# Layer 0's expert rows sorted on the chip: one expert on each tile of sorted rows in place of eight experts on each tile of tokens

## The reference

```python
x = L0_attn_x
xn = _layernorm(x, axis=-1)
x = x + _L0_attn_ref(xn, ...) + _L0_ffn_ref(xn, ...)   # linear attention, 4 heads of 32; 8 experts, top 2
xn = _layernorm(x, axis=-1)
x = x + _L1_attn_ref(xn, ...) + _L1_ffn_ref(xn, ...)   # 16 causal heads of 64; 8 experts, grouped top 2
```

```python
xn = rms_norm(x, norm_scale)
scores = (xn @ w_router.T).astype(jnp.float32)
scores_topk, idx = jax.lax.top_k(scores, TOP_K)
weights = jax.nn.softmax(scores_topk, axis=-1)
...
up = moe_linear(xf, ids, w_up)          # row i gets w_up[ids[i]]: 128 -> 512
u, gate = jnp.split(up, 2, axis=-1)
h = u * jax.nn.silu(gate)
down = moe_linear(h, ids, w_down)       # 256 -> 128
out = jnp.sum(down.reshape(B, S, TOP_K, D) * weights[..., None], axis=-2)
```

## Time and profile before

| | us |
|---|---|
| median of 3 runs (lowest, highest) | 782.28 (782.05, 784.48) |
| the profiled execution | 782.97 |
| its span, first to last instruction | 781.2 |
| busy: PE, DVE, ACT, POOL | 730.0, 594.1, 477.9, 345.8 |
| mean granted TensorE clock | 0.989 of full speed |

### The profile page before, as it was taken

The page is one execution under the profiler, slowest core; times in us unless marked ns, Lnnn a source line. Parts: engine busy times, 40 slices in busy tenths (PEclk is TensorE's granted clock), DMA queues, the critical chain, the costliest instruction groups (busy, mean ns, idle before and its releaser), DMA issues.

```text
span 781.2 us, 17355 instructions
## 1 busy us (share of the span) xinstructions
PE 730.0 (93%) x5473; PEld 595.4 (76%) x5473; DVE 594.1 (76%) x2233; ACT 477.9 (61%) x1276; POOL 345.8 (44%) x699
## 2 busy tenths in 40 slices
PE   2876799999999999999999999999999999999997
PEld 1765588887887878877888878777888778878875
DVE  3694987788777887778877887778877787877774
ACT  3536665676657665576656766576655756576554
POOL 3264552392425742274523924257522843257111
PEclk9997899999999999999999999999999999999999
DMA  9400000000000000000000000000000000000000
GB/s 319 170 7 1 0 3 1 1 2 14 2 2 1 2 15 2 2 1 15 2 2 1 2 15 1 3 1 1 16 2 2 1 8 2 2 1 1 8 2 8
DMA packets 6027, 12.49 MB, mean 16 GB/s; under 512 B 480, under 2 KB 4864, under 8 KB 5296
## 3 DMA queue, kind: packets, MB, share of 16 engines
q1 hardware_dynamic: 5936, 11.37, 4.2%
HBM read 10.32 MB, written 1.05 MB: 15 GB/s over the span
## 4 chain that ended last, share of the span: by engine, by line
PE 74%; DVE 13%; issue 4%; ACT 4%; POOL 3%; DMA 1%; DVEq 0%; SPq 0%; POOLq 0%; ACTq 0%
PE b_y L1256 12%; PE b_simA L1304 7%; PE b_pv L1333 7%; PE b_gate L1119 5%; PE b_prT L1316 4%; PE b_y L1289 4%; PE b_gate L1121 3%; PE b_gate L1120 3%; DVE th L967 3%; PE b_up L1119 3%; PE b_up L1121 3%; PE b_up L1120 2%; DVE th L975 2%; PE b_pv L1340 2%; PE b_simB L1177 2%
## 5 line engine op out<-in xcount | busy, mean ns | idle before, releaser
L527 POOL CAST pn<-prb 128x4 fp32r<-128x4 f32 x256 | 45.7, 208 | 228.1 <-DVE prb L1051 107.1
L692 ACT ACTIVATE prb<-prb,mneg 128x130 f32<-128x130 f32 (+1 forms) x256 | 113.8, 449 | 51.7 <-DVE mneg L1066 51.7
L669 ACT ACTIVATE th<-b_gate 128x512 f32<-128x512 f32 x128 | 76.5, 598 | 111.1 <-PE b_gate L1121 109.7
L1256 PE MATMUL b_y<-down,th 128*128 128x128 f32 x1024 | 140.1, 280 | 0.9 <-DVE th L975 0.5
L1256 PEld LDWEIGHTS b_y<-down,th 128*128 128x128 f32 x1024 | 126.3, 192 | 15.1 <-issue 11.5
L967 DVE SCALAR_TENSOR_TENSOR th<-th,b_gate 128x512 f32<-128x512 f32 x128 | 87.5, 684 | 34.8 <-ACT th L669 34.1
L474 POOL TENSOR_TENSOR rn<-ss,halves 128x8 f32<-128x8 f32 x64 | 105.0, 1644 | 7.0 <-DVE ss L896 7.0
L975 DVE TENSOR_TENSOR th<-b_up,th 128x512 f32<-128x512 f32 x128 | 88.1, 689 | 10.9 <-PE b_up L1121 8.1
L1119 PE MATMUL b_gate<-xf_h,up_h 128*128 128x256 f32 x256 | 85.4, 334 | 5.8 <-DVE th L967 5.4
L1119 PE MATMUL b_up<-xf_h,up_h 128*128 128x256 f32 x256 | 79.2, 309 | 0.0
L1304 PE MATMUL b_simA<-qkT 64*128 64x130 f32 (+1 forms) x256 | 75.9, 377 | 1.5 <-DVE mneg L1066 0.8
(11 more groups left out here) (200 smaller groups left out, 1748.6 us busy)
## 6 DMA issues: line engine op xcount, KB each, us to landing
qkT<-w_up SPq DMA_DIRECT2D x1, 2048.0 KB, 9.2
down<-w_dn SPq DMA_DIRECT2D x2, 1024.0 KB, 15.3
qk<-w_up SPq DMA_DIRECT2D x1, 2048.0 KB, 14.9
x_in<-x SPq DMA_DIRECT2D x8, 128.0 KB, 2.6
qkT<-w_qk SPq DMA_DIRECT2D x1, 1024.0 KB, 5.0
result<-acc SPq DMA_DIRECT2D x8, 128.0 KB, 1.9
...
```

The source lines that it names most:

```text
L669: nc.scalar.activation(th[e % 2][:], b_gate[:], ACT.Tanh, scale=0.5).then_inc(*act_moe[layer](f"th{e}"))
L692: nc.scalar.activation(prb[p % 2][:, i, 0:n], prb[p % 2][:, i, 0:n], ACT.Exp, scale=-1.0, bias=mneg[:, qt, h:h + 1], accum_out=lsum[:, qt, ...
L1256: ins = nc.tensor.matmul(b_y[:, t * D:(t + 1) * D], th[e % 2][:, a * S + t * P:a * S + (t + 1) * P], down[layer][:, e, a], start=(a == 0), ...
```

## The change

Layer 0 no longer goes by batch up to its experts. At the start all sixteen tiles of tokens are normalised and routed at once, on DVE, with the count of rows before each row by a scan and a matmul. The two rows of every token get positions in a table `sorted_rows` in device memory, where each expert's rows begin at a multiple of 128: 40 tiles (5120 rows, zeroed first), each of one expert. POOL writes the rows there by indirect DMA; layer 0's attention (`mixing`) is computed meanwhile for all batches. Then PE, ACT and DVE work through PAIRS = 20 pairs of tiles; the expert of a tile is read from `slot_expert` into a register that addresses the weights. The results go to `expert_rows`, from which four indirect DMAs per batch fetch each token's two rows again. The rounds keep heads, layer 1's experts (now at EXPERT_AT, every second step from 2 to 16) and front1 with other places; front0 is gone from them. The high and low parts of the up weights now have one buffer for both layers, so that layer 1's are split after the pairs, in front1 of batch 0.

The rounds, the constants of the order:

```diff
+EXPERT_AT = [2, 4, 6, 8, 10, 12, 14, 16]
...
-            for b in range(0, B - 2):
-                in_round(b, steps)
-            in_round(B - 2, steps, f0=False)
-            in_round(B - 1, steps, m0=False, f0=False, f1=False)
+            return lambda b, p: step(b, p) if b >= 0 else None
+
+        def front(front1, i):
+
+            return lambda b, p: front1(b + 1, 2 * p + i) if b + 1 < B else None
+
+        def all_rounds(*steps):
+            for b in range(-1, B):
+                for p in range(ROUND):
+                    for step in steps:
+                        step(b, p)
+        PROJ_AT = [10 + 3 * n for n in range(8)]
+        SQUARE_AT = [k + 1 for k in PROJ_AT]
+        ROOT_AT = [k + 2 for k in PROJ_AT]
```

SP: zeroing, and the loads and stores of pairs:

```diff
+            sp.wait_ge(zero_set, 1)
+            flat_rows = sorted_rows.rearrange("(p r) d -> p (r d)", p=P)
+            for at in range(0, ROWS * D // P, 2 * HD1):
+                n = min(2 * HD1, ROWS * D // P - at)
+                sp.dma_start(flat_rows[:, at:at + n], zeros[:, 0:n]).then_inc(zero_in, 16)
...
+            def load_rows(s):
+
+                if s >= 4:
+                    sp.wait_ge(pair_pe["turn"], s - 3)
+                sp.dma_start(rows_in[s % 4], sorted_rows[2 * s * P:2 * (s + 1) * P].rearrange("(t p) d -> p t d", p=P))\
+                    .then_inc(rows_loaded[s % 4], 16)
+
+            sp.wait_ge(scattered, 16 * 2 * TILES)
+            for s in range(4):
+                load_rows(s)
+            sp.dma_start(flat(xf_all), w_up1[:, 0:2 * QUARTER]).then_inc(up1_in[0], 16)
+            for s in range(PAIRS):
+                if s + 4 < PAIRS:
+                    load_rows(s + 4)
+                sp.wait_ge(pair_act["out"], s + 1)
+                sp.dma_start(expert_rows[2 * s * P:2 * (s + 1) * P].rearrange("(t p) d -> p t d", p=P), rows_out[s % 2])\
+                    .then_inc(rows_stored[s % 2], 16)
```

POOL: scatter, and the gathers inside the rounds:

```diff
+            pool.wait_ge(zero_in, 16 * ZEROINGS)
+            pool.wait_ge(xf_set, 2)
+            pool.wait_ge(*ROUTED("pos"))
+            for k in range(2):
+                for i in range(TILES):
+                    nc.gpsimd.indirect_dma_start(out=sorted_rows, out_offset=bass.IndirectOffsetOnAxis(ap=pos[:, k, i:i + 1], axis=0),
+                                                 in_=xf_all[:, i], in_offset=None).then_inc(scattered, 16)
+
+            pool.wait_ge(scattered, 16 * 2 * TILES)
...
+            def take_rows(b):
+
+                if b == 0:
+                    pool.wait_ge(nv_set, 1)
+                    for i in range(2):
+                        pool.wait_ge(rows_stored[i], 16 * PAIRS // 2)
+                pool.wait_ge(*dve_f1.at(b - 2, "x1"))
+                for t in range(T):
+                    for k in range(2):
+                        nc.gpsimd.indirect_dma_start(out=taken_rows[b % 2][:, t, k], out_offset=None, in_=expert_rows,
+                                                     in_offset=bass.IndirectOffsetOnAxis(ap=pos[:, k, T * b + t:T * b + t + 1], axis=0))\
+                            .then_inc(rows_taken[b % 2], 16)
+                pool.wait_ge(rows_taken[b % 2], 16 * 2 * T * (b // 2 + 1))
...
-                if 28 <= k < 36:
-
-                    n = k - 28
+                if k in (1, 4):
+                    inverse_std(b, k // 4)
+                if k == 12 and b + 1 < B:
+                    take_rows(b + 1)
+                for n in [n for n in range(8) if k == ROOT_AT[n]]:
+
                     w, t, g = piece_of(n)
                     hs = slice(g * HALF, (g + 1) * HALF)
                     pool.wait_ge(*dve_f1.at(b, f"floor{n}"))
                     nc.gpsimd.tensor_tensor(rn[:, w, t, hs], ss[:, w, t, hs], halves[:, 0:HALF], ALU.pow).then_inc(*pool_f1(f"rn{n}"))
-                    if not (isinstance(b, int) and b == 0):
+                    if b:
                         pool.wait_ge(*pool_f1.at(b, f"rn{n}"))
                         unit_vectors(nc.gpsimd, n)
```

ACT in the pair stage (its four pieces and their order):

```diff
+            def pair_input(s):
+
+                act.wait_ge(pair_pe["turn"], s + 1)
+                if s >= 2:
+                    act.wait_ge(pair_pe["up"], s - 1)
+                nc.scalar.activation(pair_h[s % 2][:], pair_T[s % 2][:, 0:2 * P], ACT.Copy).then_inc(pair_act["xh"], 1)
...
+            def pair_gate(s):
+
+                act.wait_ge(pair_pe["up"], s + 1)
+                if s >= 2:
+                    act.wait_ge(pair_pe["hidT"], s - 1)
+                nc.scalar.activation(pair_th(s), pair_half(s, 1), ACT.Tanh, scale=0.5).then_inc(pair_act["th"], 1)
...
+            for s in range(2):
+                pair_input(s)
+            for s in range(PAIRS + 2):
+                if s < PAIRS:
+                    pair_gate(s)
+                if s + 2 < PAIRS:
+                    pair_input(s + 2)
+                if s >= 2:
+                    pair_out(s - 2)
+                if 1 <= s <= PAIRS:
+                    pair_hidden(s - 1)
```

PE: routing's count, and the pair stage:

```diff
+            pe.wait_ge(*ROUTED("rank"))
+            ends = rank[:, :, TILES - 1]
+            nc.tensor.matmul(b_count[:, 0:E], below, ends, start=True, stop=True)
+            nc.tensor.matmul(b_count[:, E:2 * E], ones, ends, start=True, stop=True).then_inc(counted, 1)
...
+            def pair_ups(s):
+
+                pe.wait_ge(pair_dve["xl"], s + 1)
+                if s >= 2:
+                    pe.wait_ge(pair_dve["hid"], s - 1)
+                for t in range(2):
+                    e = pe.value_load(slot_expert[0:1, 2 * s + t:2 * s + t + 1], min_val=0, max_val=E - 1)
+                    tok = slice(t * P, (t + 1) * P)
+                    high = up_h[:, bass.ds(e, 1), :].rearrange("p e n -> p (e n)")
+                    ins = matmul3(pair_up[s % 2][:, t * 512:(t + 1) * 512], pair_h[s % 2][:, tok], pair_l[s % 2][:, tok],
+                                  high, up_l[:, bass.ds(e, 1), :].rearrange("p e n -> p (e n)"))
+                ins.then_inc(pair_pe["up"], 1)
...
+            def pair_down(s):
+
+                pe.wait_ge(pair_act["hidT"], s + 1)
+                if s >= 1:
+                    pe.wait_ge(pair_act["out"], s)
+                for t in range(2):
+                    e = pe.value_load(slot_expert[0:1, 2 * s + t:2 * s + t + 1], min_val=0, max_val=E - 1)
+                    for a in range(HB):
+                        ins = nc.tensor.matmul(b_rows[:, t * D:(t + 1) * D], hidT[s % 2][:, t * HB + a],
+                                               down[:, bass.ds(e, 1), a * D:(a + 1) * D].rearrange("p e n -> p (e n)"),
+                                               start=(a == 0), stop=(a == HB - 1), skip_group_check=True)
+                ins.then_inc(pair_pe["down"], 1)
...
+            pe.wait_ge(*ROUTED("slots"))
+            pe.wait_ge(up_lo[0], 4)
+            pe.wait_ge(dn0_in, 16)
+            for s in range(2):
+                pair_turn(s)
+            for s in range(PAIRS + 2):
+                if s < PAIRS:
+                    pair_ups(s)
+                if s + 2 < PAIRS:
+                    pair_turn(s + 2)
+                if s >= 2:
+                    pair_down(s - 2)
+                if 1 <= s <= PAIRS:
+                    pair_hidden(s - 1)
```

1322 lines of the change are left out of this document (713 added, 609 removed).

## The result

The changed kernel takes 886.91 us, median of four runs (882.98 to 894.74), against 782.38 (782.05 to 784.48): ratio 1.134, 95% interval 1.125 to 1.143. Slower was forecast, at 794 with a range up to 852; the time lies 93 us above the forecast and 35 above the range.

The account below looks back on a forecast made before the run. PE's work was taken to bound the full rounds, with chains setting start and end. First score at 230, plus rounds of 435, 70 and 57.6, gave 793, adjusted to 794 us; range 742 to 852.

Parts of the forecast that it names:

- A: Start, routing all tokens at once: loads, normalisations, logits and a DVE chain; positions stand at 33 us (bounds 30 to 38).
- B: Scatter: 32 indirect DMAs on POOL at 1.2 us each, 38.4, then landing of the last and first row load, 2.6 each.
- C: Pair stage: PE's work 3.5 us a pair plus 1.5 of register loads in the open, 5.0; 20 pairs make 100.
- D: First gathers after the pair stage: four indirect DMAs at 1.2 us and a landing of 2.6, 7.4 us.
- E: front1 of batch 0, alone: today's 32.5 us plus x1's additions 1.3 and the weight split 4, 37.8.
- F: Rounds: 63.2 us of PE work and present waits, plus 6.7 and 2.5; six with gathers 435, the one without 70.
- 7.4 against a lead of two steps: Next batch's gathers and landing in POOL's queue ahead of pn, delaying DVE's scores: 2.5 us a round (bounds 0 to 6).
- R2: Rival, slower still: indirect DMAs at 1.64 us and PE at 1.2 GHz for half the pair stage; 840 us, chance 0.20.
- 6.7 + 2.5: Added time a round: 6.7 us exposed while DVE holds the first three steps, 2.5 us of waiting for pn behind gathers.
- The last round: Final round, which had no layer-0 experts before either: taken as 57.6 us, as today.
- R1: Rival, not slower: cheap issues, indirect DMAs at 0.85 us and pairs of 4.4; 750 us, chance 0.30.
- R3: Rival: rounds stay at 83 us since chains of front1 and the heads set them, not PE; 870 us, chance 0.04.

Follow-up runs that it names:

- e8: Changed kernel with pair stores issued two pairs later and layer 0's experts as constants instead of numbers read into PE's register: 826.47 us, ratio 1.053.
- e1: Changed kernel with SP issuing the store of each pair two pairs later: 850.26 us, ratio 1.087.
- e10: Changed kernel with DVE's scaling of each q and k piece two half steps later in front1 of batch 0: 894.08 us, ratio 1.142.
- e2: Changed kernel with the next batch's gathers moved from k = 12 to k = 34 of the round: 850.99 us, ratio 1.089.
- e7: Changed kernel with 16 unused PE transposes at step 8 of each round, gathers left at k = 12: 878.30 us, ratio 1.121.
- e3: Changed kernel with 4 and 16 unused PE transposes behind the scores of steps 0 and 1 of each round: 883.81 us, ratio 1.129.
- e14: e12 with POOL pausing after every eighth scatter DMA, plus 4 and 8 unused PE transposes at each round's start: 776.64 us, ratio 0.993.
- e12: Changed kernel: stores two pairs later, DVE's scaling later, gathers at k = 8, next batch's rows added at k = 43, down reusing ups' register: 806.46 us, ratio 1.031.

## Why the prediction was wrong, step by step

*A, positions at 33:* 34.4. Right, though its own terms add up to 32.2. *B, scatter, 41 us, measured 46.2:* 32 DMAs, mostly 1.26 us apart (0.96 and 0.30 of issue between) for the 1.2 taken; five were longer, two of them here in POOL's timeline:

```profile
44.87 1.98 POOL L488 DMA_INDIRECT sorted_rows<-xf_all,pos  x1 [0.30 <-issue]
47.15 0.96 POOL L488 DMA_INDIRECT sorted_rows<-xf_all,pos  x1 [0.30 <-issue]
48.41 2.00 POOL L488 DMA_INDIRECT sorted_rows<-xf_all,pos  x1 [0.30 <-issue]
```

and DVE's of the same stretch:

```profile
44.74 1.28 DVE L964 SCALAR_TENSOR_TENSOR up_l<-bias,small,up_h 128x1024 fp32r<-128x1024 f32 x1
48.31 1.28 DVE L964 SCALAR_TENSOR_TENSOR up_l<-bias,small,up_h 128x1024 fp32r<-128x1024 f32 x1
```

The long ones start just behind DVE's 1024-column operations and take 1.98 and 2.00 us in place of 0.96. The Trainium skill (SBUF — State Buffer, the "DVE blocks DMA" trap) tells of such a wait behind DVE's two-port operations, with an fp32 copy as the example; these rows agree in kind, but show it behind operations that read two tensors. The prediction's estimate by that rule, under 4 us, comes to 4.4 over the five, and DVE's work of this kind, put at under 4 us, is six operations and 7.6 us. The last DMA landed 1.3 us after its issue ended, where 2.6 was taken; the loads of rows took 2.6 by the median, as taken.

*C, pairs of 5.0, near in its parts and wrong in the whole.* PE's 3.5 measured 2.94 (e8), in part by luck: down took 0.89 where 0.45 was written (the run of eight matmuls was halved, and a pair has all eight), while the weight sets, the turns and the waits took 2.05 for 3.05. The loads' 1.5 measured 1.16 (e1 against e8): 4.1. What failed is the step "0.9 for each less what the previous matmuls cover ... 5.0 us a pair" as a full list of what the pair waits for: SP's queue was not followed. No term stands for the rows' loads, and a load stood behind a store that waits for ACT. That is 1.7 a pair (5.81 against e1's 4.10), with the low clock in the pauses.

*D and E:* the gathers took 7.8 for 7.4. E took 44.5, and its 37.8 would have been right with e10's order (37.2); the failed step is "its chain sets its length, so I leave it at that". The spacing of the pieces changed from one half step to three, and this put the scaling of a piece ahead of the next reduction in DVE's queue. The order of the instructions showed it.

*F is where most is missing.* The step "7.4 against a lead of two steps ... less pn's own operations, 0.9: 2.5" is the term that was mis-sized: the stall is 4.9 on DVE and, with what follows from it, 36 us over six rounds by e2, 6 a round. The gathers and their landing took 7.0; the sum, but for its upper bound, had left out what stands between the landing and pn in POOL's queue, a root and a scaling, 2.7 us:

```profile
456.90 1.67 POOL L531 TENSOR_TENSOR rn<-ss,halves 128x8 f32<-128x8 f32 x1 [2.17 <-DMA taken<-expert_rows,pos]
458.65 1.04 POOL L332 TENSOR_TENSOR qk<-qk,rn 128x512 f32<-128x512 f32 x1
460.03 0.20 POOL L558 TENSOR_TENSOR pn<-prb,pn 128x4 fp32r<-128x4 f32 x1
```

The second fault is that no step of the sum has PE's clock in it: the lower level stood in R2 only, and there for the pair stage. The idle time of PE in a round was well forecast, 6.7 + 2.5 = 9.2 against 10.0 (83.0 less 73.05 busy); PE's busy time was not, 73 for some 63 of work. e7 shows 2.7 us a round of it on the path, e3 shows that at the start it lay beside DVE's chain, and e14 suggests that it comes onto the path when that chain is shorter. Nor is all of it the clock: at a granted clock of 1.00 e14's round has PE busy 67.5, of which its 12 transposes are some 1.4 (0.117 each, an estimate), so some 3 us more than forecast have another cause, which is open.

*The last round,* 57.6 taken as today, measured 62.8. Its experts stood from step 1 on and now stand in steps 2 to 16; PE is busy 55.0 in place of 51.2. No run tests it.

*Rivals.* R1 had cheap issues: wrong for the kernel as it stood, though its pair of 4.4 came near e1's 4.10. R2 named the clock, at 840, and only for the pair stage: there it was 0.86, where half of the time at the lower level would be 0.75, and more of the time at that level lay in the rounds (0.91 over 489.8 us); its indirect DMAs at 1.64 did not come. (R2's ten pairs at 2.2 are 22 and not 24.) R3, rounds that stay at 83, gave 870 and was given 0.04: the number came out, the mechanism (chains of front1 and heads set the round) did not, as e2's 74.7 shows. The ends of the range left no room for two causes of R2's kind at once.

What stays open: why the stall in the scatter comes in some series and not in others, and on the same chip. That it lies inside the scatter, is over with the last landing and shortens with pauses is shown; that the engines wait for their instructions behind the indirect DMAs is a guess from "remote" and "issue". Neither was e12's earlier start of front1 run alone.
